# Queries' RMS factors of an audio tower's attention: one Ln and Exp per item instead of one per half, and the queries' chain two slots earlier

## Chip, cores and metric

The kernel runs on one core of one Trainium2 chip. The metric is the device time of one execution in microseconds (us). The core has five engines with queues of their own that run in order: TensorE (PE), VectorE (DVE), ScalarE (ACT), GpSimd (POOL) and SyncE (SP, which only starts DMAs here). They wait for each other by semaphores.

## What is computed

Sixty-four items of 10240 samples pass through four convolutions with normalisation, an MLP that gives each of 128 positions an importance, a pooling to 64 positions by it, an attention block and a mixture of experts. The change touches the queries of the attention: 16 heads of 64 values for each of 128 tokens, turned by rotary embedding and divided by their root mean square.

```python
h = tok(x)                                       # convolutions, MLP, pooling: 64 x 128 x 64
h = h + attn(layernorm(h))
h = h + ffn(layernorm(h))                        # 8 experts, top 2

q = rmsnorm(rope(x @ wq.T), q_norm_w)            # x * rsqrt(mean(x * x) + eps) * w, for each head
k = rmsnorm(rope(x @ wk.T), k_norm_w)            # one head for all 16 queries
attn = softmax(mask(q @ k.T / 8)) @ v @ wo.T
```

## The kernel before

Attention works on 64 items. An item is one tile of 128 tokens; it has two *halves* of eight heads (half m belongs to item m // 2) and four *parts* of four heads (part n belongs to item n // 4). Four items are a *quad* and share their keys' work.

The order of all work is written out by hand in *slots*. Each engine's program is a loop over the same slots; in a slot it runs what tables such as `at_q` (L1069) say, in the order in which the engine's `slot` function asks for them. There is one attention slot for each part, so 256 of them (0 to 255), and a quad takes 16. Work that comes ahead of an item's first part stands in earlier slots, so the first items' work has negative slots. The pooling phase has slots of its own, which are the same loop: attention slot u is pooling slot u + 82, and in each slot the pooling's steps come first, then attention's, then the experts' (FFN's). The last pooling group (pooling slots 66 to 86) therefore shares the slots from -16 to 4 with the start of attention. This stretch is called the fill here. Pooling's weights (L1012, L1017, L1020, L1026 on POOL) for the last three quads stand in the slots -12, -11 and -10, its matmuls with them (L752) in -8, -7 and -6, the transposes of its input (L738, copied by ACT at L829 to hT) in -11, -10 and -9, the way back of whitened results (PE L767, ACT L833) up to slot 1. The FFN's bias terms (PE L1695, L1697) stand in slot -14.

The queries' chain of half m, for item i = m // 2 and h = m % 2, with its slots before:

- slot 4i-11+2h: `project` on PE (L1163, L1164, two matmuls into the one bank QB, after the Square of half m-1), `rope_q` on DVE (L1277 to L1279, from QB into t1 and t2), `add_q` on POOL (L1545, qr = t1 + t2). qr has two copies, by the item's parity.
- one slot later: `square` on ACT (L1417, from QB into sqb), `sum_q` on DVE (L1310, sums of eight heads into ssq).
- slot 4i-9+2h: `rms_q` on ACT, a Ln (L1423, ssq to lrq) and an Exp (L1428, lrq to rq), on the half's eight columns. ssq, lrq and rq have 16 columns and one copy (the trace calls them assq, alrq and arq).
- slot 4i-8+2h: `scale_q` on POOL (L1552, qr times rq).
- slot 4i-5+2h: `q_t` on PE (L1173, four transposes), copied by ACT one slot later (`keep_q`, L1435).
- slot 4i+2h: `scores` on PE (L1186, L1191) for two parts.

For part n: `maximum` on DVE in slot n (L1317), `exps` on ACT in slot n (L1446, four exponentials with their sums, the last step of ACT's slot), `recip` on DVE (L1325, after the maximum of slot n+1), `normalize` on POOL in slot n+1 (L1559, the first step of POOL's slot), `p_t` on PE and `p_copy` on DVE in slot n+3 (L1203, L1332), `p_v` on PE (L1214, ACT's copy L1455).

On ACT `rms_q` comes directly ahead of the odd slots' `exps`; the Exp waits until the `scale_q` that still reads these columns of rq is done (`qm`). On POOL a slot holds, in this order, `normalize`, `add_q`, `scale_q`, parts of the input's normalisation, then the keys' steps (`add_k` L1517, `square_k` L1523, `scale_k` L1529, `weigh_k` L1536). For the first quad these stand in the slots -13, -12, -9 and -8; DVE's `sum_k` (L1303) in -11 and ACT's `rms_k` (L1399, L1403) in -10. On ACT the pooling's copies come ahead of attention's steps in a slot.

Of the kernel before, what the change touches and what calls it, by code (L numbers as in the profile page):

```python
# [12 lines left out]
ACT = mybir.ActivationFunctionType  # L13
# [3 lines left out]
B = 64  # L17
# [6 lines left out]
NH, DH = 16, 64  # L24
# [1013 lines left out]
def attention_phase(nc, V, sem, ctx, kept, pool):  # L1038


    ps, K, epsc = V["ps"], V["K"], V["epsc"]
# [8 lines left out]
    def first(q):  # L1050
        return 16 * (q - 1)

    def by_slot(count, slot):
        return {slot(n): n for n in range(count)}

    PARTS = 4 * B
    HALVES = 2 * B
# [8 lines left out]
    at_kmul = by_slot(QUADS, lambda q: first(q) + 7)  # L1066
    at_kn = by_slot(QUADS, lambda q: first(q) + 8)
    at_kt = by_slot(QUADS, lambda q: first(q) + 13)
    at_q = by_slot(HALVES, lambda m: 4 * (m // 2) - 11 + 2 * (m % 2))  # L1069
    at_rms = by_slot(HALVES, lambda m: 4 * (m // 2) - 9 + 2 * (m % 2))  # L1070
    at_qm = by_slot(HALVES, lambda m: 4 * (m // 2) - 8 + 2 * (m % 2))
    at_qt = by_slot(HALVES, lambda m: 4 * (m // 2) - 5 + 2 * (m % 2))
    at_pt = by_slot(PARTS, lambda n: n + 3)
# [5 lines left out]
    def sb(name, shape, dt=F32):  # L1079
        return ctx.enter_context(nc.sbuf_tensor(name, shape, dt))  # L1080
# [19 lines left out]
    ssq = sb("assq", [T, NH])  # L1100
    lrq = sb("alrq", [T, NH])
    rq = sb("arq", [T, NH])
# [14 lines left out]
    S = {n: sem("a_" + n) for n in names}  # L1117
# [155 lines left out]
    def vector(ve):  # L1273
# [31 lines left out]
        def sum_q(m):  # L1305
            i, h = m // 2, m % 2
            ve.wait_ge(S["sq"], m + 1)
            if i >= 1:
                ve.wait_ge(S["lrq"], m - 1)
            ve.tensor_reduce(ssq[:, 8 * h:8 * h + 8], sqb[:, h, :].rearrange("p (h d) -> p h d", h=8), AX_X,  # L1310
                             ALU.add).then_inc(S["ssq"], 1)

# [50 lines left out]
        def slot(u):  # L1363
            if u == AT_SPLIT:
                prepare()
            if u == first(0):
                ve.wait_ge(made["m3"], QUADS)
            if 0 <= u < PARTS:
                maximum(u)
            if 0 <= u - 1 < PARTS:  # L1370
                recip(u - 1)
            if u in at_pt:
                p_copy(at_pt[u])
            if u in at_q:
                rope_q(at_q[u])
            if u - 1 in at_q:
                sum_q(at_q[u - 1])
            if u in at_krope:
                rope_k(at_krope[u])
            if u in at_ksum:  # L1380
                sum_k(at_ksum[u])
            if u in at_tr:
                residual(at_tr[u])
            if u - 2 in at_tr:
                statistics(at_tr[u - 2])
# [3 lines left out]
    def scalar(ac):  # L1389
        def keep_x(q):  # L1390
            ac.wait_ge(S["xt"], q + 1)
            if q >= 2:
                ac.wait_ge(S["q"], 8 * (q - 1))
                ac.wait_ge(S["kv"], q - 1)
            ac.activation(xT[:, q % 2, :], ps[:, XB, :], ACT.Copy).then_inc(S["xa"], 1)

        def rms_k(q):
            ac.wait_ge(S["kss"], q + 1)
            ac.activation(kln[:], kss[:], ACT.Ln, bias=epsc[:, 1:2], scale=1.0 / DH).then_inc(S["kln"], 1)  # L1399
            ac.wait_ge(S["kln"], q + 1)  # L1400
            if q >= 1:
                ac.wait_ge(S["km"], q)
            ac.activation(rk[:], kln[:], ACT.Exp, scale=-0.5).then_inc(S["rk"], 1)  # L1403

        def keep_k(q):
            ac.wait_ge(S["kt"], q + 1)
            if q >= 2:
                ac.wait_ge(S["s"], 16 * (q - 1))
            ac.activation(kT[:, q % 2, :, :], ps[:, XB, :].rearrange("p (r s) -> p r s", r=4), ACT.Copy
                          ).then_inc(S["kT"], 1)  # L1410

        def square(m):
            i, h = m // 2, m % 2
            ac.wait_ge(S["rope"], m + 1)
            if i >= 1:
                ac.wait_ge(S["ssq"], m - 1)
            ac.activation(sqb[:, h, :], ps[:, QB, :], ACT.Square).then_inc(S["sq"], 1)  # L1417

        def rms_q(m):
            i, h = m // 2, m % 2  # L1420
            heads = slice(8 * h, 8 * h + 8)
            ac.wait_ge(S["ssq"], m + 1)
            ac.activation(lrq[:, heads], ssq[:, heads], ACT.Ln, bias=epsc[:, 1:2], scale=1.0 / DH  # L1423
                          ).then_inc(S["lrq"], 1)
            ac.wait_ge(S["lrq"], m + 1)
            if i >= 1:
                ac.wait_ge(S["qm"], m - 1)
            ac.activation(rq[:, heads], lrq[:, heads], ACT.Exp, scale=-0.5).then_inc(S["rq"], 1)  # L1428

        def keep_q(m):  # L1430
            i, h = m // 2, m % 2
            ac.wait_ge(S["qt"], m + 1)
            if i >= 2:
                ac.wait_ge(S["s"], 4 * (i - 2) + 2 * h + 2)
            ac.activation(qT[:, i % 2, 4 * h:4 * h + 4, :], ps[:, QT, :].rearrange("p (h t) -> p h t", h=4),  # L1435
                          ACT.Copy).then_inc(S["qT"], 1)

        def exps(n):
            i, k = n // 4, n % 4
            ac.wait_ge(S["mx"], n + 1)  # L1440
            if n >= 8:
                ac.wait_ge(S["pt"], n - 7)
                ac.wait_ge(S["rc"], n - 7)
            for h in range(4):
                head = 4 * k + h
                last = ac.activation(pb[:, i % 2, head, :], ps[:, SB[n % 3], h * T:(h + 1) * T], ACT.Exp,  # L1446
                                     bias=mx[:, k, h:h + 1], accum_out=sm[:, i % 2, head:head + 1])
            last.then_inc(S["ex"], 1)

        def keep_o(m):  # L1450
            i, h = m // 2, m % 2
            ac.wait_ge(S["pv"], m + 1)
            if i >= 8 and i % 4 == 0 and h == 0:
                ac.wait_ge(S["wo"], i // 4 - 1)
            ac.activation(oT[:, i // 4 % 2, 4 * h:4 * h + 4, i % 4, :],  # L1455
                          ps[:, OB, :].rearrange("p (h t) -> p h t", h=4), ACT.Copy).then_inc(S["oT"], 1)

        def keep_y(q):
            ac.wait_ge(S["wo"], q + 1)
            if q >= 1:  # L1460
                ac.wait_ge(S["tr"], q)
            ac.activation(ysb[:], ps[:, XB, :], ACT.Copy).then_inc(S["y"], 1)

        def slot(u):
            if u == first(0):
                ac.wait_ge(made["m3"], QUADS)
            if u - 1 in at_pv:
                keep_o(at_pv[u - 1])
            if u - 1 in at_q:
                square(at_q[u - 1])  # L1470
            if u - 1 in at_qt:
                keep_q(at_qt[u - 1])
            if u in at_rms:
                rms_q(at_rms[u])
            if u in at_xt:
                keep_x(at_xt[u])
            if u in at_krms:
                rms_k(at_krms[u])
            if u - 1 in at_kt:
                keep_k(at_kt[u - 1])  # L1480
            if u - 1 in at_wo and at_wo[u - 1][1] == 3:
                keep_y(at_wo[u - 1][0])
            if 0 <= u < PARTS:
                exps(u)

        return slot

    def gpsimd(po):
# [57 lines left out]

        def scale_q(m):
            h = m % 2
            po.wait_ge(S["rq"], m + 1)
            po.wait_ge(S["qr"], m + 1)  # L1550
            q = qr[m // 2 % 2][:, h, :].rearrange("p (h d) -> p h d", h=8)
            po.tensor_tensor(q, q, rq[:, 8 * h:8 * h + 8].unsqueeze(2).to_broadcast([T, 8, DH]), ALU.mult  # L1552
                             ).then_inc(S["qm"], 1)
# [9 lines left out]
        def slot(u):  # L1563
            if u == first(0):
                po.wait_ge(made["m3"], QUADS)
            if 0 <= u - 1 < PARTS:
                normalize(u - 1)
            if u in at_q:
                add_q(at_q[u])
            if u in at_qm:  # L1570
                scale_q(at_qm[u])
            if u in at_xn:
                normal_x(*at_xn[u])
            if u in at_kadd:
                add_k(at_kadd[u])
            if u in at_ksq:
                square_k(at_ksq[u])
            if u in at_kmul:
                scale_k(at_kmul[u])
            if u in at_kn:  # L1580
                weigh_k(at_kn[u])
# [515 lines left out]
def tokens_phase(nc, V, out, sem):  # L2097
# [4 lines left out]
    with ExitStack() as ctx:  # L2102
# [5 lines left out]
        with ExitStack() as early:  # L2108
            pool = importance_pool_phase(nc, V, sem, early)
        experts = (sb("fw1l", [2 * DH, E, HID], F32R), sb("fxs", [T, 4, 4, 2, DH], F32R), sb("fgF", [64, 2, 4 * C]))  # L2110
        att = attention_phase(nc, V, sem, ctx, kept, pool)
        ffn = ffn_phase(nc, V, out, sem, ctx, att, experts)
        slots = range(pool["first"], ffn["last"] + OFFSET)
# [129 lines left out]
```

## Time and profile before

| | us |
|---|---|
| median of 3 runs | 1932.19 |
| lowest and highest run | 1931.29 and 1932.20 |
| profiled execution, whole | 1930.25 |
| span of its trace | 1928.3 |

| engine | busy us | share of the span | instructions |
|---|---|---|---|
| PE | 1816.9 | 94% | 10533 |
| DVE | 1525.3 | 79% | 3372 |
| ACT | 1354.8 | 70% | 3865 |
| POOL | 921.0 | 48% | 1544 |

A view is an answer of the trace of this one execution. The shares are averages over stages: convolutions to about 720 us, the MLP and most of the pooling to about 1000, the fill to about 1036 (first exponentials of attention), attention to about 1745, then the experts. In a timeline each row is one instruction, or a few of the same kind in a row (x4), with its start and its duration in us from the span's start; what stands in brackets is idle time of the engine just before it and the instruction of another engine that ended it. Durations of neighbours overlap a little, so the time that an instruction takes from its engine is read from one start to the next.

### The profile page before, as it was taken

To read this page: it belongs to the slowest core of one execution; us is meant where nothing else is said; L and a number is where in the kernel's file an instruction comes from. 1 tells how busy PE (TensorE), PEld (TensorE's weight loads), DVE (VectorE), ACT (ScalarE), POOL (GpSimd) and SP (SyncE) were. 2 spreads that over 40 slices of the span, in tenths; PEclk is the share of its full clock that TensorE was granted. 3 is DMA by queue.
4 is the path that set the end of the run, shared out by engine and by line. 5 is a ranking of instruction groups with operands and counts; after the bars stand their busy time and mean duration, and the time that the engine had idled before them with its cause. 6 is when DMAs were issued, how large, how long until landed. Compare 5 with 4: busy or idle time off the path is not lost.

```text
span 1928.3 us, 35012 instructions
## 1 busy us (share of the span) xinstructions
PE 1816.9 (94%) x10533; PEld 1276.7 (66%) x10533; DVE 1525.3 (79%) x3372; ACT 1354.8 (70%) x3865; POOL 921.0 (48%) x1544
## 2 busy tenths in 40 slices
PE   3999999999999968999997999999999999999998
PEld 2777888888878856877875666666655555664443
DVE  5788888888888856566657888888999988896665
ACT  1567667767767653444436999999998999986765
POOL 1222322322322210022247989988888899983200
PEclk9999999999999988999987999999999999999999
DMA  3311111111111000000000000000000000004554
GB/s 97 96 45 38 34 47 37 35 49 34 37 47 34 25 1 1 0 1 1 1 1 1 2 2 2 2 2 2 1 2 2 2 2 2 2 2 181 188 214 166
DMA packets 30518, 69.02 MB, mean 36 GB/s; under 512 B 14108, under 2 KB 14748, under 8 KB 28028
## 3 DMA queue, kind: packets, MB, share of 16 engines
q1 hardware_dynamic: 30332, 66.78, 10.7%
q8 instruction: 87, 1.43, 0.3%
q14 instruction: 99, 0.81, 0.1%
HBM read 45.12 MB, written 2.36 MB: 25 GB/s over the span
## 4 chain that ended last, share of the span: by engine, by line
PE 37%; DVE 12%; issue 6%; POOL 4%; ACT 3%; DVEq 0%; POOLq 0%; ACTq 0%
PE ps L1191 4%; PE ps L65 4%; PE ps L1203 3%; PE ps L67 3%; PE ps L66 3%; PE ps L1224 3%; PE ps L1762 3%; PE ps L1214 2%; DVE amx L1317 2%; PE ps L1186 2%; DVE apT L1332 2%; PE ps L1173 2%; DVE assq L1310 1%; POOL apb L1559 1%; DVE atq L1277 1%
## 5 line engine op out<-in xcount | busy, mean ns | idle before, releaser
L1446 ACT ACTIVATE apb<-ps,amx 128x128 f32<-128x128 f32 x1024 | 360.0, 366 | 47.0 <-DVE amx L1317 46.5
L1559 POOL TENSOR_TENSOR apb<-apb,arc 128x512 f32<-128x512 f32 x256 | 268.4, 1048 | 43.9 <-DVE arc L1325 43.6
L1317 DVE TENSOR_REDUCE amx<-ps 128x4 f32<-128x512 f32 x256 | 174.4, 681 | 59.7 <-PE ps L1191 58.5
L1446 ACT ACTIVATION_READ_ACCUMULATOR apb<-ps,amx 128x1 f32 x1024 | 210.4, 205 | 0.0
L583 POOL TENSOR_TENSOR h0h<-h0h,const 128x1 fp32r<-128x1 f32 x256 | 46.6, 217 | 338.8 <-DVE h0l L479 338.8
L65 PE MATMUL ps<-h0h,w123h 128*128 128x512 f32 x512 | 203.0, 396 | 0.0
L67 PE MATMUL ps<-h0h,w123l 128*128 128x512 f32 x512 | 202.5, 396 | 0.0
L66 PE MATMUL ps<-h0l,w123h 128*128 128x512 f32 x512 | 202.5, 395 | 0.0
L1203 PEld LDWEIGHTS ps<-const,apb 128*128 128x128 f32 x1024 | 107.3, 140 | 135.9 <-DVE apT L1332 109.6
L479 DVE SCALAR_TENSOR_TENSOR h0l<-ps,h0h 128x1024 fp32r<-128x1024 f32 x128 | 156.0, 1219 | 46.3 <-ACT h0h L383 46.3
L1203 PE MATMUL ps<-const,apb 128*128 128x128 f32 x1024 | 167.6, 286 | 18.7 <-DVE apT L1332 18.0
L1332 DVE COPY apT<-ps 128x512 f32<-128x512 f32 x256 | 170.0, 664 | 6.8 <-PE ps L1203 6.5
L1191 PEld LDWEIGHTS ps<-akT,aqT 64*128 64x128 f32 x2048 | 125.0, 188 | 54.7 <-issue 54.7
L1191 PE MATMUL ps<-akT,aqT 64*128 64x128 f32 x2048 | 149.6, 286 | 0.0
L383 ACT ACTIVATE h0h<-ps 128x1024 fp32r<-128x1024 f32 x128 | 129.9, 1015 | 24.9 <-PE ps L307 24.9
L1214 PE MATMUL ps<-apT,avs 128*64 128x512 f32 x512 | 136.6, 612 | 0.0
L807 ACT ACTIVATE z<-ps,mcol 128x512 f32<-128x512 f32 x64 | 44.1, 689 | 114.8 <-PE ps L67 114.8
L1012 POOL TENSOR_TENSOR part<-cs,const 128x512 f32<-128x512 f32 x16 | 18.3, 1142 | 214.5 <-DVE cs L925 213.2
L67 PEld LDWEIGHTS ps<-h0h,w123l 128*128 128x128 f32 x512 | 97.0, 189 | 22.5
L66 PEld LDWEIGHTS ps<-h0l,w123h 128*128 128x128 f32 x512 | 97.4, 190 | 18.8
L1830 ACT ACTIVATE apb<-ps,mw 128x512 f32<-128x512 f32 x128 | 81.0, 687 | 40.8 <-PE ps L1749 40.5
L65 PEld LDWEIGHTS ps<-h0h,w123h 128*128 128x128 f32 x512 | 97.0, 189 | 18.8 <-DVE sq1b L498 0.4
(320 smaller groups left out, 5065.9 us busy)
## 6 DMA issues: line engine op xcount, KB each, us to landing
h<-gates SPq DMA_DIRECT2D x8, 2048.0 KB, 7.1
atq<-gates SPq DMA_DIRECT2D x8, 2048.0 KB, 7.3
x0k<-x0h SPq DMA_DIRECT2D x128, 72.0 KB
x<-in_x SPq DMA_DIRECT2D x32, 192.0 KB, 2.6
x0k<-x0l SPq DMA_DIRECT2D x64, 72.0 KB
x0k<-x0h SPq DMA_DIRECT2D x64, 48.0 KB
out<-akT SPq DMA_DIRECT2D x16, 128.0 KB, 1.9
x0k<-x0l SPq DMA_DIRECT2D x32, 48.0 KB
```

What stands on the lines that cost most here:

```text
L65: pe.matmul(out, wh, xh, start=start, stop=False)
L66: pe.matmul(out, wh, xl, start=False, stop=False)
L67: return pe.matmul(out, wl, xh, start=False, stop=stop)
L383: ac.activation(padded(h0h, row, half, i), ps[:, Y0:Y0 + 2, :], ACT.Relu).then_inc(s_h0h, 1)
L479: ve.scalar_tensor_tensor(out=padded(h0l, row, half, i), in0=ps[:, Y0:Y0 + 2, :], scalar=0.0, in1=padded(h0h, row, half, i).bitcast(F32), ...
L1191: last = pe.matmul(bank[:, p * T:(p + 1) * T], qT[rows, i % 2, 4 * h + p, :], kT[rows, i // 4 % 2, i % 4, :], start=False, stop=True, skip ...
L1203: last = pe.transpose(ps[:, TB, h * T:(h + 1) * T], pb[:, i % 2, 4 * k + h, :], K["ident"])
L1214: last = pe.matmul(ps[64 * odd:64 * odd + 64, OB, :], vs[:, i // 4 % 3, i % 4, :], pT[:, 8 * h + 4 * odd:8 * h + 4 * odd + 4, :], start=Tr ...
L1317: ve.tensor_reduce(mx[:, n % 4, :], ps[:, SB[n % 3], :].rearrange("p (h s) -> p h s", h=4), AX_X, ALU.max, negate=True).then_inc(S["mx"], 1)
L1332: ve.tensor_copy(pT[:, 4 * k:4 * k + 4, :], ps[:, TB, :].rearrange("p (h t) -> p h t", h=4)).then_inc(S["pT"], 1)
L1446: last = ac.activation(pb[:, i % 2, head, :], ps[:, SB[n % 3], h * T:(h + 1) * T], ACT.Exp, bias=mx[:, k, h:h + 1], accum_out=sm[:, i % 2, ...
L1559: po.tensor_tensor(p, p, rc[:, i % 2, 4 * k:4 * k + 4].unsqueeze(2).to_broadcast([T, 4, T]), ALU.mult).then_inc(S["pn"], 1)
```

## The change

The queries' chain up to the sums starts two slots earlier (`at_q`, slot 4i-13+2h; the Square and the sums follow in the slot after it, as before). `rms_q` runs once for an item, in slot 4i-9, on all 16 columns: one Ln and one Exp where there were two of each. Its Exp waits until both halves of the item before are scaled. The scaling, the transposes and everything behind them keep their slots.

```diff
-    at_q = by_slot(HALVES, lambda m: 4 * (m // 2) - 11 + 2 * (m % 2))
-    at_rms = by_slot(HALVES, lambda m: 4 * (m // 2) - 9 + 2 * (m % 2))
+    at_q = by_slot(HALVES, lambda m: 4 * (m // 2) - 13 + 2 * (m % 2))
+    at_rms = by_slot(B, lambda i: 4 * i - 9)
...
             if i >= 1:
-                ve.wait_ge(S["lrq"], m - 1)
+                ve.wait_ge(S["lrq"], i)
...
-        def rms_q(m):
-            i, h = m // 2, m % 2
-            heads = slice(8 * h, 8 * h + 8)
-            ac.wait_ge(S["ssq"], m + 1)
-            ac.activation(lrq[:, heads], ssq[:, heads], ACT.Ln, bias=epsc[:, 1:2], scale=1.0 / DH
-                          ).then_inc(S["lrq"], 1)
-            ac.wait_ge(S["lrq"], m + 1)
+        def rms_q(i):
+            ac.wait_ge(S["ssq"], 2 * i + 2)
+            ac.activation(lrq[:], ssq[:], ACT.Ln, bias=epsc[:, 1:2], scale=1.0 / DH).then_inc(S["lrq"], 1)
+            ac.wait_ge(S["lrq"], i + 1)
             if i >= 1:
-                ac.wait_ge(S["qm"], m - 1)
-            ac.activation(rq[:, heads], lrq[:, heads], ACT.Exp, scale=-0.5).then_inc(S["rq"], 1)
+                ac.wait_ge(S["qm"], 2 * i)
+            ac.activation(rq[:], lrq[:], ACT.Exp, scale=-0.5).then_inc(S["rq"], 1)
...
-            po.wait_ge(S["rq"], m + 1)
+            po.wait_ge(S["rq"], m // 2 + 1)
             po.wait_ge(S["qr"], m + 1)
```

## Rows read from the trace of the kernel before

**Rows 1.** Stretches: busy us of PE, PEld, DVE, ACT, POOL; clock, DMA share, GB/s.

```profile
1257.29:1301.27 43.98, 43.17 (x328) 26.55 (x324) 38.87 (x96) 40.23 (x175) 39.46 (x41) 1.00 0.00 1
1010.00:1020.00 10.00, 5.88 (x24) 3.94 (x24) 5.20 (x17) 4.06 (x10) 9.66 (x11) 0.50 0.00 0
```

**Rows 2.** Waits, 1125.4 to 1389.28 (six quads): us in total, times, longest.

```profile
DVE amx L1317 <- PE ps L1191: 22.1, 18, 1.6
...
PE ps L1203 <- DVE apT L1332: 4.9, 12, 0.7
...
DVE arc L1325 <- ACT apb L1446: 3.1, 6, 0.5
```

**Rows 3.** Timeline of ACT around slot 87, a Ln, its Exp and what follows.

```profile
1275.17 0.31 ACT L1423 ACTIVATE alrq<-assq,epsc 128x8 f32<-128x8 f32 x1
1275.51 0.21 ACT L1428 ACTIVATE arq<-alrq 128x8 f32<-128x8 f32 x1
1275.63 0.35 ACT L1446 ACTIVATE apb<-ps,amx 128x128 f32<-128x128 f32 x1
```

**Rows 4.** Timeline of POOL in the fill, slots -13 to -10.

```profile
1004.97 0.72 POOL L1517 TENSOR_TENSOR akr<-aka,akb 128x256 f32<-128x256 f32 x1 [15.63 <-DVE akb L1279]
1005.65 1.04 POOL L1012 TENSOR_TENSOR part<-cs,const 128x512 f32<-128x512 f32 x1
...
1009.65 0.61 POOL L1523 TENSOR_TENSOR aks<-akr 128x256 f32<-128x256 f32 x1
...
1014.23 1.26 POOL L1545 TENSOR_TENSOR atq<-atq 128x512 f32<-128x512 f32 x1
1015.45 1.04 POOL L1012 TENSOR_TENSOR part<-cs,const 128x512 f32<-128x512 f32 x1
```

**Rows 5.** Timelines of PE and DVE in the fill, slots -13 to -6.

```profile
1009.11 0.69 PE L767 MATMUL ps<-const,wx 128*128 128x128 f32 x2
...
1011.28 0.78 PE L1163 MATMUL ps<-wh,axx 128*128 128x512 f32 x1
...
1015.51 1.09 PE L738 MATMUL ps<-const,h 128*128 128x128 f32 x4 [2.08 <-issue]
...
1023.13 1.12 PE L752 MATMUL ps<-hT,wm 128*64 128x128 f32 x8
...
1012.52 0.69 DVE L1277 TENSOR_TENSOR atq<-ps,const 128x512 f32<-128x512 f32 x1 [1.07 <-PE ps L1164]
```

**Rows 6.** Timelines of ACT and PE in the fill, slots -9 and -1 to 0.

```profile
1014.83 0.58 ACT L829 ACTIVATE hT<-ps 128x512 f32<-128x512 f32 x1
...
1033.00 0.21 ACT L1428 ACTIVATE arq<-alrq 128x8 f32<-128x8 f32 x1
1033.12 0.55 ACT L833 ACTIVATE h<-ps,par 128x256 f32<-128x256 f32 x1
...
1033.81 0.41 PE L767 MATMUL ps<-const,wx 128*128 128x128 f32 x2 [0.58 <-ACT h L833]
```

**Rows 7.** Timelines of POOL and DVE around slots 86 to 88.

```profile
1274.98 1.05 POOL L1552 TENSOR_TENSOR aqr<-aqr,arq 128x512 f32<-128x512 f32 x1
...
1278.80 0.17 DVE L1325 RECIPROCAL arc<-asm 128x4 f32<-128x4 f32 x1
```

**Rows 8.** Timelines of POOL and ACT around slot 15.

```profile
1079.52 1.05 POOL L1552 TENSOR_TENSOR aqr<-aqr,arq 128x512 f32<-128x512 f32 x1
...
1078.26 0.21 ACT L1428 ACTIVATE arq<-alrq 128x8 f32<-128x8 f32 x1
```

**Rows 9.** Timelines of POOL and ACT around slot 235, PE and DVE around 243.

```profile
1688.87 1.07 POOL L1552 TENSOR_TENSOR atq<-atq,arq 128x512 f32<-128x512 f32 x1
...
1687.74 0.21 ACT L1428 ACTIVATE arq<-alrq 128x8 f32<-128x8 f32 x1
...
1708.96 0.48 PE L1163 MATMUL ps<-wh,axx 128*128 128x512 f32 x1
1709.27 0.40 PE L1164 MATMUL ps<-wl,axx 128*128 128x512 f32 x1
...
1712.50 0.69 DVE L1317 TENSOR_REDUCE amx<-ps 128x4 f32<-128x512 f32 x1 [1.30 <-PE ps L1191]
```

## Prediction, made before the changed kernel ran

> **What bounds the kernel now.** I read the busy time by stretch first, then the table of waits, then the timelines of single engines. A quad here is 16 slots of attention, that is four items. In the middle of attention a quad takes 43.98 us, and every engine is nearly full in it: matmuls busy 43.17, ACT 40.23, POOL 39.46, DVE 38.87 us [rows 1]. So busy shares don't name the bound; the waits do. Over six quads DVE waits 22.1 us for the scores' matmuls, the PE waits (its matmuls idle) 4.9 us for DVE's copies of apT, and DVE's reciprocals wait for ACT's exponentials in 6 cases of 96, 3.1 us [rows 2]. The chain of a quad, followed in the timelines, runs PE (scores) to DVE to PE to DVE to PE and never needs an ACT instruction to be earlier. ACT's own idle time there ends with DVE's maxima. Before that, from about 1000 to 1036 us, lies the fill: the pooling phase's last slots and the attention's first (negative) slots share the engines, POOL is busy 9.66 us of 10, the PE runs at a granted clock of 0.50, which is 1.2 GHz, and is busy only 5.88 [rows 1]. That stretch is a chain of latencies with POOL's pooling weights in it, and what is put into it lengthens it.
>
> **The change, part by part.**
>
> *1. ACT does less.* A Ln and its Exp take ACT from 1275.17 to 1275.63, 0.46 us [rows 3]. 128 such pairs become 64: 64 x 0.46 = 29 us less ACT work. All of it lies in slots u = 4i-7, odd ones. After an odd slot's exponentials the reciprocal is not near: the exponentials that start at 1275.63 take four times about 0.34 us and end at 1277.0, the reciprocal that reads their sums starts at 1278.80 [rows 3, 7], after DVE waited for the PE. An ACT that is 0.46 us earlier there moves nothing. The even slots, where ACT is sometimes last, do not change. I take 0 us; the bound for a gain is the wait for ACT in the table, 3.1 us in six quads, about 8 us over 16 [rows 2].
>
> *2. The new wait.* arq has one copy. Before, the Exp for half m waited for the scaling (scale_q, L1552) of half m-2, three slots back. Now the Exp of item i waits until both halves of item i-1 are scaled, and the second of these stands in POOL's slot just before. Behind the Exp on ACT stand the four exponentials of the slot, and DVE's reciprocal waits for them. In steady quads the scaling ends between 0.05 us before and 0.52 us after the old start of that Exp. The pair shown: scaling at 1274.98, next POOL instruction 1.00 later, so done at 1275.98; old Exp at 1275.51 [rows 3, 7]. With 0.05 us for the semaphore the slot's exponentials start at 1276.15 and not 1275.63, and end near 1277.5. The reciprocal at 1278.80 still finds them done. The other three items of the quad have less to wait or nothing. So 0 us in the steady quads; if nothing covered it, 0.57 + 0.34 us for each quad, 11 us in 12 quads.
>
> Where POOL lags the wait is longer. At the start of attention (slot 15) the scaling starts at 1079.52 and ends 2.3 us after the old Exp at 1078.26 [rows 8]; item 5 before it lacks 1.5 us. Following the slots forward, reciprocals come 1.0 and 1.65 us late, and with them the apT copies that the PE waits for: the PE loses 0.65, then 0.45 more. I take +1.1 us (0 to 2.3). Near the end POOL also normalises the FFN's input; the Exp of slot 235 at 1687.74 would wait for a scaling that starts at 1688.87 [rows 9], 2.2 us, with three neighbours lacking 2.0, 1.9 and 0.7. Reciprocal and copy slip by 0.9 to 1.4 us, DVE's waits for the PE take up part. I take +1.2 us (0 to 3).
>
> *3. The chain two slots ahead, at the end.* The last projection leaves slot 243. On the PE it stands at 1708.96 and 1709.27, 0.55 us, directly ahead of the scores that DVE waits 1.30 us for at 1712.50, and from there DVE is busy without a break [rows 9]; its sum of squares in slot 244, 0.6 us, goes as well. That is -1.15 us, nearly what the waits near the end cost.
>
> *4. The chain two slots ahead, in the fill.* Here one more half is started, and its place is bad. Projection 0 moves from slot -11 to -13, behind the transposes at 1009.11 on the PE, because the FFN's bias terms (slot -14) keep the PE busy until then [rows 5]. It starts near 1009.5. From a projection's start to DVE's rope is 1.24 us here (1011.28 to 1012.52) [rows 5], the rope takes 1.3, so t1 and t2 are there at 1012.1. In POOL's slot -13 add_q stands ahead of add_k and of the pooling weights. In the trace before, add_k starts at 1004.97 and the first weights at 1005.65 [rows 4]. Now POOL waits until 1012.1, adds (1.23), adds k (0.7) and starts the weights at 1014.05, **8.4 us late**. Weights are 4.0 us each (1005.65 to 1009.65), square_k 0.57, an add_q 1.22 between [rows 4]: the third set ends at 1027.85, not at 1019.45.
>
> What hides part of it: the pooling matmul that needs the third set ran at 1023.13 [rows 5], so this path is late by 4.75 us. The second path gives the same: sum_k on DVE waits for square_k, now at 1018.6, ACT's Ln for k and then the copy of hT (before at 1014.83) follow at 1019.55, and the PE's transposes, before at 1015.51, go at 1020.2 [rows 5, 6]. **+4.75 us.** Then the new wait again, on a POOL with 8.4 us of lag against 4.75 elsewhere. From 1027.85 POOL has add_q, scale_k, scale_q(0), weigh_k, add_q, scale_q(1), about 1.2 + 0.6 + 1.0 + 1.25 + 1.2 + 1.0 = 6.3 us, so scale_q(1) ends at 1034.1, and the Exp of item 1 (slot -5), due at 1030.7, stands for 3.4 us. Behind it on ACT is the Square of the next projection, and the PE's next projection waits for that Square: it slips 1.6 us more. The Exp of item 2 (slot -1) loses 1.65 again: it stood at 1033.00, directly ahead of the pooling's relu at 1033.12, for which the PE idles 0.58 us ahead of the first scores [rows 6]. **+1.6 and +1.65.** Sum of the fill: +8.0 us; bounds 0 (if the fill hides everything) and 8.4 + 3.3 = 11.7.
>
> The other queues: PE, DVE and POOL keep the order of their instructions from slot -11 on, only with the half one further. add_q(m) now waits for the transposes of half m-4 in its own slot, but it also waits for rope(m), 1.3 us of DVE work behind the same projection, while the transposes take 0.45; so 0 us. No DMA moves.
>
> *Sum*: 8.0 + 1.1 + 0 + 1.2 - 1.15 = +9.1 us. On the profiled execution (span 1928.3, whole 1930.25, 1.9 below the median of the runs) that is 1939.4; on the median 1932.19 it is **1941 us**.
>
> **A rule against this reading.** The rows say that matmuls are busy 43.17 of 43.98 us while weight loads are busy 26.55 [rows 1]. The Trainium skill, "Perfetto Trace Analysis", section "Identifying the Most-Contended Engine", says that matmul busy time doesn't show how near the PE is to its limit, that busy weight loads do, and that the engine with the highest occupancy is to be relieved first; by 26.55 us the PE would have room and ACT, at 91%, would be the one. By that rule the sum would be near 1907; by the rows' waits it is 1941.
>
> **Rivals.**
> *A, forecast:* as above, 1936 to 1946. For it: POOL's weights run without a gap, and the order in the queues is fixed. Chance 0.60.
> *B, the wait bites in steady quads too:* the 0.57 and 0.34 us are not covered, because another late engine has used the slack of the reciprocals. 12 quads x 0.91 = 11 us more: 1952; half of it 1946. Against it: 6 waits of 96 for ACT [rows 2]. Chance 0.14.
> *C, the fill hides it:* the PE idles at 1015.51 for 2.08 us [rows 5] and in four more places after it; if those gaps rather than the weights set the fill, the 8 us shrink to 0 to 3, and the total lies at 1931 to 1935. It decides for this side if the third weights' end stays before the matmul's turn, that is if POOL's start slips by less than 3.7 us. Chance 0.18, a fifth of it faster by over 0.2%.
> *D, ACT is the bound, the other side:* the steady quad follows ACT's load. 4 x 0.46 of 40.23 us is 4.6%, of 43.98 us that is 2.0 us for each quad, 32 us for 16: 1932.2 + 9 - 32 = 1909; a quarter of that relief, with the fill's cost at 5, gives 1929. It decides from where ACT's relief in odd slots brings the even slots' exponentials forward. Against it: ACT's waits end with DVE's maxima. Chance 0.08.
>
> **The numbers.** A measurement of this kernel can tell 0.2%, 3.9 us. Slower: A and B, 0.74. Same: most of C, 0.14. Faster: D and the rest of C, 0.12. The range 1931 to 1949 leaves out D, the lowest of C and the upper half of B and a little of A, 0.2 together.
>
> **What the changed profile would show.** If part 4 is right: POOL's first weights (L1012 in the fill) start about 8 us later against the transposes before them, with an add_q ahead that waited for DVE; the first scores of attention come some 8 us later; ACT has idle time ahead of the Exp of arq, released by POOL. If part 1 is right, the steady quad stays at 43.97 us with ACT busy near 38.3. B would show quads of 44.5 or more; D quads below 43; C first scores within 3 us of before. The prediction is wrong if the order of the queues around slot -13 is not as I read it, or if the clock of 1.2 GHz lasts longer in the stretched fill, which would add.

## Result, and the profile after

| | before | after |
|---|---|---|
| median us | 1932.2 | 1943.0 |
| lowest and highest | 1931.3 to 1933.1 | 1938.1 to 1945.3 |
| profiled execution, whole | 1930.25 | 1942.85 |
| span of its trace | 1928.3 | 1940.9 |
| ACT busy us, instructions | 1354.8, 3865 | 1331.5, 3737 |

The ratio is 1.0053, with a 95% interval of 1.0041 to 1.0066: slower by 10.8 us, clear of the 0.2% that a measurement can tell. A second set of runs gave 1943.3 against 1931.3, 1.0064 (1.0051 to 1.0076). The forecast was 1941 and a range of 1931 to 1949.

First the steady quads. This is the busy time of the quad from slot 80 to 96 after the change (us of PE, PEld, DVE, ACT, POOL; clock, DMA share, GB/s), and under it the waits of six quads from slot 32 on (us in total, times, longest).

```profile
1268.74:1312.72 43.98, 42.84 (x322) 26.55 (x324) 38.91 (x96) 38.83 (x167) 39.47 (x41) 1.00 0.00 1
```

```profile
DVE amx L1317 <- PE ps L1191: 20.5, 18, 1.6
...
ACT arq L1425 <- POOL aqr L1549: 6.8, 12, 0.7
...
DVE arc L1325 <- ACT apb L1443: 4.7, 6, 0.8
```

The quad takes 43.98 us as in [rows 1]; ACT has less to do in it (38.83 against 40.23). ACT now stands for POOL's scaling twice in each quad, 0.41 and 0.74 us, and nobody behind it is later in the end: DVE's wait for ACT grew from 3.1 to 4.7 us in six quads, its wait for the PE fell from 22.1 to 20.5 [rows 2].

Now the fill. First the PE (lines behind the edit are three lower now: L1545 is L1542, L1552 is L1549, the Exp L1428 is L1425), then POOL in its own timeline.

```profile
1009.22 0.69 PE L767 MATMUL ps<-const,wx 128*128 128x128 f32 x2
1009.56 0.77 PE L1163 MATMUL ps<-wh,axx 128*128 128x512 f32 x1
```

```profile
1012.29 1.28 POOL L1542 TENSOR_TENSOR atq<-atq 128x512 f32<-128x512 f32 x1 [22.84 <-DVE atq L1279]
1013.53 0.73 POOL L1514 TENSOR_TENSOR akr<-aka,akb 128x256 f32<-128x256 f32 x1
1014.22 1.04 POOL L1012 TENSOR_TENSOR part<-cs,const 128x512 f32<-128x512 f32 x1
```

The first projection stands behind the transposes that follow the bias terms; POOL stands until 1012.29; the pooling weights start at 1014.22, 8.6 us later than in [rows 4]. And ACT, in the slots -5 and -1, with the PE at the first scores:

```profile
1034.43 0.22 ACT L1425 ACTIVATE arq<-alrq 128x16 f32<-128x16 f32 x1 [3.20 <-POOL atq L1549]
...
1041.37 0.21 ACT L1425 ACTIVATE arq<-alrq 128x16 f32<-128x16 f32 x1 [1.34 <-POOL aqr L1549]
1041.49 0.55 ACT L833 ACTIVATE h<-ps,par 128x256 f32<-128x256 f32 x1
...
1042.19 0.61 PE L767 MATMUL ps<-const,wx 128*128 128x128 f32 x2 [1.93 <-ACT h L833]
...
1043.58 2.08 PE L1191 MATMUL ps<-akT,aqT 64*128 64x128 f32 x16
```

Both Exps stand for POOL, and the relu (L833) that the PE waits for stands behind the second: 1041.49 against 1033.12 [rows 6], 8.4 us late. The scores' matmuls (L1191) behind it take 2.08 us, at a granted clock of 1.2 GHz. In a second execution of the same kernel they ran at 2.4 GHz:

```profile
1043.68 1.16 PE L1191 MATMUL ps<-akT,aqT 64*128 64x128 f32 x16
```

To compare kernels I use marks: the start of the first exponential of a slot, counted from ACT's first copy to axx (slot -16, at 1000.50 before), less the same in the kernel before. The column "relu" is the same for the relu just ahead of slot 0. The count from slot -16 is needed, because the stages ahead of it differ by up to 4.4 us between these executions. The marks of a kernel are of one profiled execution, so the column "end" is not the difference of medians, which stands last.

| kernel | relu | slot 0 | 10 | 24 | 224 | 248 | end | median minus before |
|---|---|---|---|---|---|---|---|---|
| changed | 8.3 | 9.8 | 9.8 | 11.1 | 11.4 | 12.4 | 12.5 | +10.8 |
| changed, again | 7.9 | 7.9 | 9.2 | 10.4 | 10.7 | 11.8 | 11.9 | +12.0 |
| shift only | 4.8 | 5.2 | 3.7 | 3.6 | 3.5 | 3.0 | 3.0 | +4.4 |
| wait only | 0.9 | 0.9 | 2.2 | 3.3 | 3.5 | 5.0 | 5.0 | +6.2 |
| changed, two copies of arq | 4.8 | 5.0 | 2.6 | 2.7 | 2.6 | 2.1 | 2.1 | +2.2 |
| changed, first add later | 3.5 | 3.5 | 3.4 | 4.1 | 4.4 | 5.4 | 5.5 | +7.3 |
| both of these | 1.5 | 1.5 | 2.3 | 2.3 | 2.3 | 1.8 | 1.8 | +1.2 |
| both, add behind the square | 2.0 | 2.0 | 1.6 | 1.7 | 2.8 | 2.3 | 2.3 | +2.1 |
| changed, bias terms later | 5.1 | 6.7 | 6.6 | 7.3 | 7.5 | 8.6 | 8.7 | +8.6 |
| all three | -0.4 | -0.4 | -0.4 | -0.5 | -0.5 | -1.0 | -1.0 | -0.9 |
| half of the pairs left out | 0.0 | 0.0 | -0.1 | -0.1 | -0.1 | -0.1 | -0.1 | -0.3 |
| more Exps on ACT | 0.0 | 0.0 | 2.9 | 2.7 | 2.8 | 2.8 | 2.8 | +0.8 |

The PE's clock takes part in these marks. From the relu to slot 0, 3.74 us in the kernel before, it adds 1.6 us in the first trace of the changed kernel and in the one with the bias terms later (5.3 us at a mean granted clock of 0.68), and nothing in the changed kernel's second trace (3.75 us at 1.00); with the shift alone it is 0.4 us (4.13 us at 0.85). In the slots 0 to 2 it moves the marks by -1.5 to +1.6 us (the last section has the figures). So the delay of the fill is read at the relu.

### The profile page after: what moved, and what is told of

It reads as the page before. It is cut to its first block, busy times and chain, and to the rows that moved or that the text cites. A ratio compares the mean times of both kernels' runs of the same rounds, so it can differ in the third digit from the quotient of the medians.

```text
span 1940.9 us, 34757 instructions
## 1 busy us (share of the span) xinstructions
PE 1814.0 (93%) x10469; PEld 1277.8 (66%) x10533; DVE 1527.2 (79%) x3372; ACT 1331.5 (69%) x3737; POOL 922.3 (48%) x1544
## 4 chain that ended last, share of the span: by engine, by line
PE 31%; DVE 10%; POOL 10%; issue 8%; ACT 3%; DVEq 0%; POOLq 0%; ACTq 0%
PE ps L65 4%; PE ps L67 3%; POOL apb L1556 3%; PE ps L66 3%; PE ps L1191 3%; PE ps L1759 3%; PE ps L1203 2%; PE ps L1224 2%; DVE amx L1317 2%; PE ps L1214 1%; DVE apT L1332 1%; PE ps L1745 1%; POOL aqr L1542 1%; PE ps L1186 1%; DVE atq L1277 1%
## 5 line engine op out<-in xcount | busy, mean ns | idle before, releaser
L1443 ACT ACTIVATE apb<-ps,amx 128x128 f32<-128x128 f32 x1024 | 365.1, 383 | 36.5 <-DVE amx L1317 36.2
L1443 ACT ACTIVATION_READ_ACCUMULATOR apb<-ps,amx 128x1 f32 x1024 | 227.3, 222 | 0.0
L1191 PEld LDWEIGHTS ps<-akT,aqT 64*128 64x128 f32 x2048 | 125.9, 189 | 55.1 <-issue 55.1
L1191 PE MATMUL ps<-akT,aqT 64*128 64x128 f32 x2048 | 150.6, 287 | 0.0
```

The costliest lines, as they stand in the source:

```text
L1191: last = pe.matmul(bank[:, p * T:(p + 1) * T], qT[rows, i % 2, 4 * h + p, :], kT[rows, i // 4 % 2, i % 4, :], start=False, stop=True, skip ...
```

## Experiments

**Shift only.** The kernel before with one line of the change.

```diff
-    at_q = by_slot(HALVES, lambda m: 4 * (m // 2) - 11 + 2 * (m % 2))
+    at_q = by_slot(HALVES, lambda m: 4 * (m // 2) - 13 + 2 * (m % 2))
```

> The kernel before with only the projections, sums and additions two slots earlier; Ln and Exp stay per half in their old slots, each waiting for the scaling three slots back. My theory: the cost is a chain of two causes, POOL's late pooling weights in the fill (8.5 us late start, 4.75 us of it visible) and the new wait of the Exp. Here only the first is left: the weights on POOL start 8.5 us late, the first exponentials come 5 to 7 us late (less than the 9.9 of the changed kernel), quads stay at 43.97 us, slots 0 to 16 lose nothing, the end gains 1.1: 1936 to 1938 us. Rival, the new wait is all of the cost: 1931 to 1932 us. Rival, the earlier chain is all of it: 1943 us as in the changed kernel.

1935.96 us against 1931.58, 1.0024 (1.0015 to 1.0033). POOL stands as in the changed kernel:

```profile
1014.01 1.27 POOL L1545 TENSOR_TENSOR atq<-atq 128x512 f32<-128x512 f32 x1 [22.84 <-DVE atq L1279]
...
1015.93 1.04 POOL L1012 TENSOR_TENSOR part<-cs,const 128x512 f32<-128x512 f32 x1
```

(This execution reached the stretch 1.7 us later than the changed kernel's.) The relu is 4.8 us late and the first exponentials 5.2, nothing is lost in slots 10 to 24, and the end gains 0.5, not 1.1. The shift is 4.4 of the 10.8 us; neither rival holds.

**Wait only.** The kernel before with the other half of the change's effect.

```diff
             if i >= 1:
-                ac.wait_ge(S["qm"], m - 1)
+                ac.wait_ge(S["qm"], m - h)
```

> The kernel before with nothing but the new wait: the Exp of an item's first half waits for the scaling of both halves of the item before, not of the first alone. My theory: in the fill, without POOL's lag, the Exp of items 1 and 2 stands for 0.6 and 1.2 us, so the first exponentials come 0.5 to 1.5 us late; slots 11 to 16 lose 1 to 1.5 us, the steady quads nothing, the end 1 to 2 us: 1934.5 to 1937 us. Together with the shift alone (+4.4 us by the medians) that leaves 2 to 4 us of the changed kernel's 10.8 to the two at once. Rival, the wait bites in each quad: 1940 us or more. Rival, the wait by itself is hidden: 1932 us.

1937.19 against 1931.01, 1.0033 (1.0020 to 1.0045). In the fill the two Exps stand for 0.76 and 1.35 us, with POOL's weights on time:

```profile
1026.83 0.21 ACT L1428 ACTIVATE arq<-alrq 128x8 f32<-128x8 f32 x1 [0.76 <-POOL atq L1552]
...
1034.12 0.21 ACT L1428 ACTIVATE arq<-alrq 128x8 f32<-128x8 f32 x1 [1.35 <-POOL aqr L1552]
```

The marks lose 0.9 to slot 0, 1.1 in slots 10 to 24 and 1.5 from 224 to 248; the quads stay at 43.97. The 1.4 us lost in the slots 0 to 2 go with the clock there, 0.64 against 0.79 before. I had expected 2 to 4 us to belong to the two halves of the change at once. The medians don't show it, 4.4 + 6.2 = 10.6 of 10.8 us, but they can't rule it out either: each of the three is known to within 1.7 to 2.4 us, and against the 12.0 of the second set 1.4 us are left. The relu shows it: 4.8 us late with the shift, 0.9 with the wait, 8.3 and 7.9 with both, so 2.2 to 2.6 us belong to the two at once. The place is the Exp in slot -5, which stands for 3.20 us in place of 0.76.

**Two copies of arq.** The changed kernel without its new wait.

```diff
-    rq = sb("arq", [T, NH])
+    rq = sb("arq", [T, 2, NH])
...
-            if i >= 1:
-                ac.wait_ge(S["qm"], 2 * i)
-            ac.activation(rq[:], lrq[:], ACT.Exp, scale=-0.5).then_inc(S["rq"], 1)
+            if i >= 2:
+                ac.wait_ge(S["qm"], 2 * i - 2)
+            ac.activation(rq[:, i % 2, :], lrq[:], ACT.Exp, scale=-0.5).then_inc(S["rq"], 1)
...
-            po.tensor_tensor(q, q, rq[:, 8 * h:8 * h + 8].unsqueeze(2).to_broadcast([T, 8, DH]), ALU.mult
+            po.tensor_tensor(q, q, rq[:, m // 2 % 2, 8 * h:8 * h + 8].unsqueeze(2).to_broadcast([T, 8, DH]), ALU.mult
```

> The changed kernel with two copies of arq, by the item's parity, so that the Exp waits for the scaling of the item before last. My theory: the same time as the shift alone within 1 us (1936 to 1938 us), no idle time of ACT ahead of the Exp, first exponentials 5 to 7 us late, 0 in slots 11 to 16 in place of 1.5 us, and the end no later than before. Rival, the waits cost nothing because other work is late anyway: 1943 us. Rival, ACT's relief pays once nothing makes it wait (64 pairs less, 29 us of ACT): below 1930 us and quads below 43.9 us.

1933.74 against 1931.58, 1.0012 (1.0003 to 1.0021): the wait is worth 8.6 us in the changed kernel, and the result lies 2 us under what I expected. ACT's idle time ahead of the 64 Exps is gone. The marks show half of the 2 us: the first exponentials are nearly as late as with the shift alone (5.0 and 5.2), but from slot 0 to 10 this kernel makes up 2.4 us and the other 1.5. The 0.9 us between them lie in the slots 2 to 10, most of it in 4 and 5. It looks like a gain from the ACT work saved, but it goes with the clock. These are the slots 4 and 5 of the shift alone, of this kernel, and of the run below in which the pairs are left out (columns as above):

```profile
1056.57:1062.27 5.70, 5.39 (x34) 3.93 (x36) 4.60 (x12) 4.77 (x23) 5.70 (x7) 0.70 0.01 1
```

```profile
1056.95:1061.96 5.01, 4.67 (x36) 2.93 (x36) 4.83 (x12) 4.37 (x22) 5.01 (x7) 1.00 0.01 2
```

```profile
1050.59:1056.35 5.76, 5.45 (x34) 4.08 (x36) 4.61 (x12) 4.46 (x22) 5.76 (x7) 0.70 0.01 1
```

With less ACT work and a clock of 0.70 the two slots are as long as with all of it. No run shows a gain from the ACT work saved.

**The first half's addition behind the first weights.**

```diff
-            if u in at_q:
+            if u in at_q and at_q[u] > 0:
                 add_q(at_q[u])
+            if u - 1 in at_q and at_q[u - 1] == 0:
+                add_q(0)
```

> The changed kernel with one POOL instruction moved: the first half's addition stands in slot -12 behind the first set of pooling weights, not in slot -13 ahead of it. My theory: the weights start again at 1005.7, the first exponentials come 0 to 2.5 us late (what the new wait costs by itself in the fill), the losses of 1.5 us in slots 11 to 16 and of 1.1 near the end stay: 1934 to 1937 us. Rival, the fill is late because of one more half in it, wherever it stands: 1941 to 1943 us.

1938.84 against 1931.58, 1.0036 (1.0024 to 1.0049). POOL's weights start on time and then POOL stands all the same:

```profile
1008.77 0.72 POOL L1514 TENSOR_TENSOR akr<-aka,akb 128x256 f32<-128x256 f32 x1 [15.59 <-DVE akb L1279]
1009.45 1.04 POOL L1012 TENSOR_TENSOR part<-cs,const 128x512 f32<-128x512 f32 x1
...
1015.92 1.27 POOL L1542 TENSOR_TENSOR atq<-atq 128x512 f32<-128x512 f32 x1 [2.42 <-DVE atq L1279]
```

The rope of half 0 was so late that an addition after 4 us of weights still waits 2.42 us for it. The fill's delay at the relu falls from 8.3 to 3.5 us, and the losses of the wait (slots 10 to 24, and near the end) stay. The time is 2 us above my range, and the 3.5 us are above the 0 to 2.5 that I had given the fill: something in it besides POOL's weights is late.

**Both.** The two edits above together.

> The changed kernel with both: two copies of arq, and the first half's addition behind the first set of weights. My theory: nothing is left of the cost, and the end gains up to 1.1 us: 1930 to 1933 us, the same as before, with 29 us less work on ACT. Rival, ACT's load matters: 1925 us or less. Rival, some cost of the earlier chain in the fill is left on PE or DVE: 1934 to 1937 us.

1932.74 against 1931.58, 1.0008 (0.9999 to 1.0016), not told from no change. The marks still say 1.5 at slot 0.

**Both, and the addition behind the keys' square.**

```diff
             if u in at_ksq:
                 square_k(at_ksq[u])
+            if u - 1 in at_q and at_q[u - 1] == 0:
+                add_q(0)
```

> The changed kernel with two copies of arq, and the first half's addition on POOL in slot -12 behind the keys' square too, not only behind the first weights. In the run with it ahead of the square POOL stood 2.42 us for the rope with the square, and so the keys' sum on DVE and Ln on ACT, behind it. My theory: the first exponentials come within 0.7 us of the kernel before (counted from the PE's last transposes ahead of the bias terms), the end gains 0.5: 1930.5 to 1932 us, at most equal to the kernel before. Rival, the extra projection and rope in the fill cost on PE and DVE: 1933 us or more.

The addition now stands behind the square in slot -12; as in the run before, it is left out of slot -13. 1933.12 against 1931.01, 1.0012 (1.0003 to 1.0021); 2.0 us late at slot 0. My guess that the square behind the addition was the rest was wrong. (The 1.2 us that its marks lose between the slots 24 and 224 lie in one quad, 47.40 us at a clock of 0.96 where the kernel before takes 46.15 at 1.00.) DVE's timeline points at the projection itself:

```profile
1011.28 0.69 DVE L1277 TENSOR_TENSOR atq<-ps,const 128x512 f32<-128x512 f32 x1 [3.89 <-PE ps L1164]
```

DVE, in order, stands 3.89 us for a projection that stands behind the bias terms on the PE; its statistics and sums queue up behind.

**Bias terms one slot later.** First the changed kernel with this edit alone, then with the two copies and the addition behind the square as well ("all three").

```diff
-    at_bias = FIRST + 8
+    at_bias = FIRST + 9
...
-    at_weight = {FIRST + 7: 0, FIRST + 10: 5}
+    at_weight = {FIRST + 7: 0, FIRST + 11: 5}
```

> The changed kernel with the FFN's bias terms on the PE one slot later (-13), behind the first projection, and what DVE does with them one slot later too. The first projection need not stand behind them: by the rows it starts near 1006.3 and not 1009.6, POOL's weights near 1010.8 and not 1014.2. My theory: POOL's lag is the smaller part of the fill's cost and the Exp's wait on a lagging POOL the larger, so 3.4 us less lag give 2 to 4 us back: 1939 to 1941 us. Rival, the lag doesn't matter: 1943 us, as the changed kernel.

1939.84 against 1931.27, and 1943.29 for the changed kernel in the same set: 3.5 us back. Counted from slot -16, POOL's weights start 3.1 us earlier than in the changed kernel, and the relu and the first exponentials too.

```profile
1008.48 1.27 POOL L1542 TENSOR_TENSOR atq<-atq 128x512 f32<-128x512 f32 x1 [19.73 <-DVE atq L1279]
...
1010.39 1.04 POOL L1012 TENSOR_TENSOR part<-cs,const 128x512 f32<-128x512 f32 x1
```

> Two copies of arq, the first half's addition behind the first weights and the keys' square, and the bias terms behind the first projection. In the run without the last of these the first exponentials were 2.0 us late with nothing of POOL's lag left, and DVE stood 3.9 us for the first projection. My theory: that was the bias terms; the first exponentials come within 0.7 us of the kernel before, the end is 0.5 us earlier: 1930 to 1932 us, the same as before. Rival, one more projection, rope, square and sum in the fill cost 2 us wherever they stand: 1933 us.

1930.40 against 1931.27, 0.9996 (0.9987 to 1.0005): the change without its costs is the kernel before, to what can be measured. It still merges the pairs, so this is also what the merge is worth. By its marks it is 0.4 us ahead at slot 0 and 1.0 at the end. The 0.4 us are not a gain of the order: counted from slot -16, the fill's second pooling matmuls (L752) start 2.0 us late without the edit of the bias terms and 0.0 us late here (this execution is 1.5 us later at slot -16). They take 0.66 us here (second row) where they take 1.12 in the kernel before (first row): in this execution the clock was at 2.4 GHz for a stretch of the fill, and the third set starts 0.5 us early.

```profile
1020.93 1.12 PE L752 MATMUL ps<-hT,wm 128*64 128x128 f32 x8 [2.43 <-DVE pm L939]
```

```profile
1022.45 0.66 PE L752 MATMUL ps<-hT,wm 128*64 128x128 f32 x8 [2.89 <-DVE pm L939]
```

POOL no longer stands for the addition:

```profile
1011.15 0.61 POOL L1520 TENSOR_TENSOR aks<-akr 128x256 f32<-128x256 f32 x1
1011.73 1.26 POOL L1542 TENSOR_TENSOR atq<-atq 128x512 f32<-128x512 f32 x1
```

> The changed kernel once more, on the chip of the two runs above, so that they are compared with it and not with a run of another hour. My theory: 10 to 12 us over the kernel before, with the same marks as in its first trace: weights at 1014 us, first exponentials 9 to 10 us late, 1 to 2 us more in slots 11 to 16, quads of 43.97 us, 1 us more near the end. Rival, the runs' spread of 7 us has another cause than the fill: marks that differ in the steady quads.

1943.29 against 1931.27, 1.0064; the marks of this execution are in the table. At the relu it lies 0.3 us from the first one. The first one then loses 1.6 us to slot 0 at a clock of 0.68, this one 1.4 us more than the first in the slots 0 to 2; from slot 10 on the two run 0.6 to 0.8 us apart.

**Is ACT's load worth anything?** Two runs on the kernel before, less work and more work in just the slots of the merged pairs. The first leaves out the Ln and Exp of the second halves from item 1 on, so its output is not the reference's.

```diff
...
+            if h == 1 and i >= 1:
+                return
...
```

> The kernel before without the Ln and Exp of the second halves from item 1 on (those heads keep the factors of item 0, so half of the queries' normalisation is left out); ACT has 29 us less to do in just the slots in which the change relieves it, and no new wait. My theory: nothing is gained, quads stay at 43.97 us: 1931 to 1932.5 us. Rival, ACT is the bound: quads of 42 to 43 us and 1905 to 1920 us.

1930.75 against 1931.01, 0.9996 (0.9988 to 1.0005).

```diff
...
+            if h == 1:
+                ac.activation(xq[:, 0:8], lrq[:, heads], ACT.Exp, scale=-0.5)
...
+                ac.activation(xq[:, 24:32], lrq[:, heads], ACT.Exp, scale=-0.5)
```

> The kernel before with four more small Exps (128x8) in each odd slot 4i-7, about 0.48 us for each item, 31 us of ACT work more, written to a tile that nobody reads. My theory: odd slots have the room, because the reciprocal behind them waits for DVE and the PE: 1932 to 1935 us, quads up by no more than 0.2 us. Rival, ACT is the bound: quads of 45.9 us and 1960 us.

1931.76 against 1931.01, 1.0002 (0.9993 to 1.0011). The same quads in both (us as above; first the one with pairs left out, then the one with Exps added):

```profile
1257.00:1301.00 44.00, 42.85 (x322) 26.54 (x324) 38.91 (x96) 38.96 (x166) 39.52 (x41) 1.00 0.00 1
```

```profile
1257.00:1301.00 44.00, 42.86 (x322) 26.59 (x325) 38.94 (x97) 41.32 (x190) 39.48 (x41) 1.00 0.01 2
```

ACT is busy 38.96 or 41.32 us, and the slots 64 to 80 take 43.94 and 43.97 us. ACT is not the bound there; the rival that it is would have moved a quad by 2 us. Both runs move ACT's work in odd slots alone, as the change does; an even slot, where DVE at times waits for ACT, was not tried. Ahead of the steady quads the added work may cost something: this trace is 2.9 us late by slot 10, but its clock was lower there too (0.69 from slot 0 to 6, against 0.83 before), and by the medians the run is 0.8 us from the kernel before, within the noise.

## Why the prediction was right, point by point

- *What bounds (rows 1 and 2):* right. Quads from slot 32 to 224 take what they took, with the pairs merged, left out, or with more.
- *Part 1, ACT does less, 0 us:* right. All three edits together end 0.9 us below the kernel before by medians, within the noise. The relief itself was taken too large: ACT's busy time falls by 23.3 us, not 29, and to 38.83 us in a quad, not 38.3. Nothing hangs on it.
- *Part 2, the wait in steady quads, 0 us:* right. Exponentials are later by the waits, reciprocals absorb it.
- *Part 2, slots 11 to 16, +1.1 us:* the Exps of items 5 and 6 stand for 1.61 and 0.90 us after the change (the first row below is item 5's), and the marks move by 1.3 and 1.2 from slot 10 to 24 in the two traces. Right in place and size. The second row is item 61's, of slot 235, for the next point.

```profile
1079.95 0.22 ACT L1425 ACTIVATE arq<-alrq 128x16 f32<-128x16 f32 x1 [1.61 <-POOL atq L1549]
...
1701.33 0.22 ACT L1425 ACTIVATE arq<-alrq 128x16 f32<-128x16 f32 x1 [2.32 <-POOL atq L1549]
```

- *Part 2, near the end, +1.2, and part 3, -1.15:* the waits are there (2.32 us in slot 235, forecast 2.2; 2.09 in slot 231). The wait alone costs 1.5 us there, the shift alone gives 0.5. The term that was most mis-sized is part 3: the projection and the sum that leave free 1.15 us of PE and DVE, and only half of it reaches the end. Together +1.0 to 1.1 us where +0.05 stood.
- *Part 4, the fill, +8.0 us:* right in mechanism and in size. Projection at 1009.56 (forecast 1009.5), weights at 1014.22 (1014.05), Exp waits of 3.20 and 1.34 us (3.4 and about 1.7). The relu came 8.3 and 7.9 us late in the two executions. The part put down to POOL's lag alone, 4.75, measures 4.8 at the relu with the shift alone and with two copies; the waits, +3.25, are what is left, 3.1 to 3.4. The first exponentials came 9.8 and 7.9 us late; the difference between these is the PE's clock from the relu on.
- *The clock, at which the prediction put nothing:* it named a longer stretch at 1.2 GHz as something that would add, and gave it no size. Between the relu and slot 10 the two traces of the changed kernel are 1.6 and 1.3 us slower than the one of the kernel before. With only one trace of the kernel before it stays open how much of that belongs to the change and how much to the execution.
- *The rule of the Trainium skill:* by "Perfetto Trace Analysis", section "Identifying the Most-Contended Engine", weight loads of 26.55 us in a quad leave the PE room and ACT's occupancy makes it the engine to relieve. ACT's occupancy was moved between 38.8 and 41.3 us and the quad did not move; here the measurement decides against relieving the engine of high occupancy. What the rows of waits said held. (The 1907 us that the prediction gives for this rule, and the 1909 of rival D, are the same 32 us taken from 1939.4 and from 1941.)

In sum: 9.1 us were forecast, 10.8 and 12.0 measured by medians, 12.5 and 11.9 by the marks. Of the 3 us that the marks have more, 1.3 to 1.6 lie between the relu and slot 10, where the clock acts, 1.0 at the end, up to 0.2 in the slots 11 to 16 and 0.3 from there to slot 224; the fill up to the relu has within 0.3 us what was forecast. The time lies inside the range by the mechanism and not by luck: no large errors cancelled.

## What to carry to other kernels

In a hand-ordered pipeline a step that is moved earlier is put ahead of other work in every in-order queue, and in the fill its input may be far from ready: look at what already stands in the slot it moves to, on each engine. Merging two small steps into one that serves both halves makes it wait for the later half of everything that it overwrites; a second copy of a buffer of 64 bytes in each partition took that away, 8.6 us here. And where engines are all near 90% busy, work taken off one of them can be worth nothing if its waits end with another engine, as here in the odd slots: two runs, one with less and one with more of it, say so in a way that busy shares can't.

## What the runs showed of the hardware that was not expected

The PE's granted clock in the slots 0 to 2 differs from execution to execution of nearly the same work, and sets their length. The stretch from the first exponential of slot 0 to that of slot 2, in the kernel before, the shift alone, the changed kernel's first and second trace and the run with both edits (length, then busy us of PE, PEld, DVE, ACT, POOL, and the clock):

```profile
1036.86:1044.94 8.08, 5.98 (x40) 5.12 (x41) 4.73 (x25) 5.29 (x24) 2.31 (x2) 0.79 0.01 3
```

```profile
1043.90:1050.46 6.56, 4.46 (x40) 3.77 (x41) 4.71 (x25) 5.29 (x23) 3.31 (x4) 1.00 0.01 4
```

```profile
1046.80:1054.97 8.17, 6.07 (x40) 5.22 (x41) 4.69 (x25) 4.89 (x21) 2.31 (x2) 0.79 0.01 3
```

```profile
1046.00:1055.50 9.50, 7.44 (x40) 6.17 (x41) 4.67 (x25) 4.86 (x22) 2.32 (x2) 0.64 0.01 3
```

```profile
1037.79:1047.50 9.71, 7.61 (x39) 6.28 (x39) 4.71 (x25) 4.89 (x21) 2.32 (x2) 0.57 0.01 3
```

The same 40 matmuls take 4.46 us at 2.4 GHz throughout and 7.61 with most of the stretch at 1.2 GHz; in all five the PE waits 2.6 us for ACT's relu, until 2.1 us into the stretch. The third and fourth row are one and the same kernel, and 1.3 us apart. Between the kernels the clock moves the stretch by 3.2 us. For scale, the runs of the kernel before lie between 1929.7 and 1933.7 in one set of 27; that the clock is what spreads them is not shown, since only one of its executions was traced. A cost of 1 or 2 us in the fill can only be read from marks with the clock beside them, or from medians of many runs. Whether the changed kernel's wider spread in its first set (1938.1 to 1945.3) is this too was not tried; in the second set it was 1943.1 to 1944.0.
